# Turning and normalising the next block's rows later in a fused attention and mixture-of-experts kernel

## The reference

```python
scores = jnp.einsum('ti,ei->te', xt, gate_w)
probs = jax.nn.softmax(scores, axis=-1)
expert_weights, expert_indices = jax.lax.top_k(probs, NUM_ACT)
expert_weights = expert_weights / expert_weights.sum(axis=-1, keepdims=True)
x1 = jax.nn.silu(jnp.einsum('ti,eoi->teo', xt, w1))
x3 = jnp.einsum('ti,eoi->teo', xt, w3)
expert_outs_all = jnp.einsum('teo,eio->tei', x1 * x3, w2)
```

## Time and profile before

| | |
|---|---|
| median of 3 runs | 804.17 us (804.14 to 805.19) |
| profiled execution, its own time | 806.62 us |
| its span, first to last instruction | 804.9 us |
| mean granted TensorE clock | 0.945 of full speed |
| TensorE products busy | 729.1 us, 91% |
| VectorE busy | 412.8 us, 51% |
| ScalarE busy | 305.1 us, 38% |
| GpSimd busy | 172.6 us, 21% |

### The profile page before, as it was taken

How to read it: one execution, slowest core, us unless ns; L and a number is a source line. 1 busy time by engine, 2 the same in 40 slices (tenths; PEclk the granted TensorE clock), 3 DMA queues, 4 the chain that set the end, 5 groups by cost and what they waited for, 6 DMA issues and landing times.

```text
span 804.9 us, 10568 instructions
## 1 busy us (share of the span) xinstructions
PE 729.1 (91%) x3364; PEld 574.8 (71%) x3365; DVE 412.8 (51%) x1011; ACT 305.1 (38%) x497; POOL 172.6 (21%) x224
## 2 busy tenths in 40 slices
PE   7393089889999999999999999999999999999995
PEld 3193054566787888788887888888888888888884
DVE  3988977885382226522282256322832563274222
ACT  4754636711362126311272255211722452172121
POOL 2353001992111111111111111111121111111211
PEclk9755579999999999999999999999999999999998
DMA  8962043664174113711174228111652182111121
GB/s 290 389 245 104 0 181 136 223 224 136 33 252 129 27 26 105 260 26 26 26 230 151 37 39 323 30 26 26 192 186 39 27 324 41 26 26 26 33 39 34
DMA packets 23103, 94.52 MB, mean 117 GB/s; under 512 B 4336, under 2 KB 4592, under 8 KB 19248
## 3 DMA queue, kind: packets, MB, share of 16 engines
q1 hardware_dynamic: 14496, 70.54, 23.7%
q0 software_dynamic: 8448, 23.81, 14.5%
q10 hardware_dynamic: 144, 0.00, 0.0%
HBM read 74.02 MB, written 20.33 MB: 117 GB/s over the span
## 4 chain that ended last, share of the span: by engine, by line
issue 68%; DVE 14%; POOL 7%; PE 5%; POOLq 3%; DVEq 2%; DMA 1%; ACT 0%; SPq 0%
POOL out L482 5%; DVE front L1002 2%; POOL xtile L443 2%; PE bank L566 1%; POOLq L479 1%; POOLq L289 1%; DVE top L1104 1%; PE bank L575 1%; PE bank L526 1%; DVE ln_stats L960 1%; DVE front L1101 1%; DVE scratch L977 1%; PE bank L564 1%; DVE xb L1155 1%; DMA front<-ctxT 1%
## 5 line engine op out<-in xcount | busy, mean ns | idle before, releaser
L621 PE MATMUL bank<-w_hi,xT_hi 128*128 128x512 f32 x560 | 225.0, 402 | 0.6 <-DVE xT_lo L1344 0.6
L623 PE MATMUL bank<-w_lo,xT_hi 128*128 128x512 f32 x560 | 221.4, 395 | 0.0
L622 PE MATMUL bank<-w_hi,xT_lo 128*128 128x512 f32 x560 | 221.3, 395 | 0.0
L898 ACT ACTIVATE act_g<-bank 128x512 f32<-128x512 f32 x70 | 41.6, 594 | 279.1 <-PE bank L623 279.1
L623 PEld LDWEIGHTS bank<-w_lo,xT_hi 128*128 128x128 f32 x560 | 105.4, 188 | 25.4
L621 PEld LDWEIGHTS bank<-w_hi,xT_hi 128*128 128x128 f32 x560 | 105.5, 188 | 24.9 <-issue 0.8
L622 PEld LDWEIGHTS bank<-w_hi,xT_lo 128*128 128x128 f32 x560 | 105.6, 189 | 23.2
L621 PE MATMUL bank<-w_hi,hT_hi 128*128 128x512 f32 x280 | 115.8, 414 | 4.8 <-DVE hT_lo L1360 4.6
L1360 DVE TENSOR_TENSOR hT_lo<-bank,hT_hi 128x512 fp32r<-128x512 f32 x70 | 48.3, 690 | 125.6 <-ACT hT_hi L902 123.2
L1164 DVE TENSOR_TENSOR w_lo<-raw,w_hi 128x1024 fp32r<-128x1024 f32 x88 | 103.9, 1221 | 14.4 <-ACT w_hi L810 13.4
L623 PE MATMUL bank<-w_lo,hT_hi 128*128 128x512 f32 x280 | 109.7, 392 | 0.0
(11 more groups left out here) (227 smaller groups left out, 714.9 us busy)
## 6 DMA issues: line engine op xcount, KB each, us to landing
raw<-weights SPq DMA_DIRECT2D x24, 2048.0 KB, 7.6
xb<-x SPq DMA_DIRECT2D x4, 1024.0 KB, 13.1
raw<-xT SPq DMA_DIRECT2D x4, 1024.0 KB, 9.8
w_hi<-weights POOLq DMA_DIRECT2D x2, 2048.0 KB, 13.9
found<-xb SPq DMA_DIRECT2D x4, 1024.0 KB, 4.7
out<-xb SPq DMA_DIRECT2D x4, 1024.0 KB, 7.6
found<-scratch SPq DMA_DIRECT2D x1, 2092.0 KB, 30.1
front<-ctxT SPq DMA_DIRECT2D x4, 256.0 KB, 5.2
```

What stands on the lines that cost most here:

```text
L621: nc.tensor.matmul(out_ap, hi, hi_w, start=start, stop=False)
L622: nc.tensor.matmul(out_ap, lo, hi_w, start=False, stop=False)
L623: return nc.tensor.matmul(out_ap, hi, lo_w, start=False, stop=stop)
L898: nc.scalar.activation(act_g[:, s, :], bank[GATE[s]][:, :], ACT.Silu).then_inc(silu_set[s], 1)
```

## The change

On all three engines the loops' order is changed, and nothing is added or taken away. TensorE turns the next block's rows four chunks before the block's end (ahead of chunk 4, before its wait for `hT_set[1]`) instead of before chunk 0. ScalarE normalises them behind `h_high(0)` in a plain block (behind `h_high(1)` in a block of a change) instead of behind `silu(0)`, and makes x's high part behind `h_high(1)`. VectorE makes x's low part behind `h_low(1)`. In a block of a change some of the weights' splits change places with these.

```diff
                     for c in range(2, DC):
                         first_layer(1, 1, c).then_inc(piece_done[1], 1)
-                    transpose_x(nth + 1)
                     pe.wait_ge(hT_set[0], nth)
...
                     second_layer([2, 3]).then_inc(piece_done[2], 1)
+                    transpose_x(nth + 1)
                     pe.wait_ge(hT_set[1], nth)
...
                         silu(0, nth)
-                        normal_x(nth + 1)
                         fresh_high(0, 3, done)
...
                         h_high(0, nth)
                         fresh_high(1, 2, done)
+                        fresh_high(1, 3, done)
+                        h_high(1, nth)
+                        normal_x(nth + 1)
+                        act.wait_ge(raw_in[2], arrived)
+                        fresh_high(2, 0, done)
                         x_high(nth + 1)
-                        h_high(1, nth)
-                        fresh_high(1, 3, done)
-                        act.wait_ge(raw_in[2], arrived)
-                        for j in range(OPS):
+                        for j in range(1, OPS):
                             fresh_high(2, j, done)
                     with act.Else():
                         silu(0, nth)
-                        normal_x(nth + 1)
                         silu(1, nth)
                         h_high(0, nth)
+                        normal_x(nth + 1)
+                        h_high(1, nth)
                         x_high(nth + 1)
-                        h_high(1, nth)
...
                         product(1, nth, ups)
+                        split_low(1, e, [2])
+                        h_low(1, nth)
+                        split_low(1, e, [3])
                         x_low(nth + 1)
-                        h_low(1, nth)
-                        split_low(1, e, range(2, OPS))
-                        split_low(2, after, range(2))
+                        split_low(2, after, [0])
                         scale_y(e, g, ups)
                         take_meta()
-                        split_low(2, after, range(2, OPS))
+                        split_low(2, after, range(1, OPS))
                     with dve.Else():
                         product(0, nth, ups)
                         h_low(0, nth)
                         product(1, nth, ups)
+                        h_low(1, nth)
                         x_low(nth + 1)
-                        h_low(1, nth)
                         scale_y(e, g, ups)
```

## The result

The changed kernel is **slower**: 816.37 us (815.81 to 816.82, 4 runs) against 804.68 us for the kernel before (4 runs, 804.14 to 806.14: the three from before the prediction and one more). The ratio is 1.0142, with a 95% interval of 1.0124 to 1.0160, so 10 to 13 us. (In brackets behind a median stand the lowest and the highest time.) The forecast was 811.6, with a range up to 816.3; the median lies 0.07 us above that end, inside the 1 us by which the changed kernel's runs scatter.

What follows compares the result with a forecast made beforehand. TensorE, busy in 91% of the span, was taken as the bound. 33 blocks x 0.37 = 12.2 us, less 4.69 gained, is +7.5; against the timed median 804.17 that gave 811.6 us, range 808.7 to 816.3.

Steps and rivals of the forecast that it cites:

- Step 1: Ahead of the second layer: without the turns of x, TensorE newly waits 0.23 us for h_low(0), gaining only 0.13 a block.
- Step 2: Behind that new wait: slower steps up to the turning of h cost 0.04 us; h's second half waits for nothing.
- Step 3: At the turns' new place, four chunks from the block's end: interrupting the dense stream costs 0.46 us a block.
- The bound of 0.41: High end of the cost per block, in us, if steps behind the interruption are also 0.04 slower; 0.37 was taken.
- Step 4: At the next block's start: the later work on x still ends in time, slack 0.82 us, hence no stall.
- The gain: Blocks behind a change of expert: with normal_x behind h_high(0), late gathers delay nothing, so all 4.69 us go.
- Steps 5 and 6: Blocks of a change, and POOL and SP: reordered splits, scale_y up to 0.8 us and loads up to 1.2 earlier; no term.
- A: Faster: h_low(0) is in time and the turns cost no more at the new place; 799.5 us, chance 0.07.
- B: Smaller: turns disturb the dense stream less, 0.23 or 0.32 us a block; 804.1 or 807.1 us, chance 0.06.
- C: Slower still: x's low part misses the next block's start, stalling each block 0.36 us; 823.5 us, chance 0.04.
- D: Turns of x wait for normal_x behind very late gathers, losing part of 4.69 us; 816.3 at most; 0.83 including the forecast.

Runs made afterwards that it cites:

- idle turns: Kernel before with four unused, unwaited turns of h's first half added four chunks from the block's end: 819.75 us; with eight, one run: 832.81 us.
- the cure alone: Kernel before with only one VectorE edit: one split of group 2 instead of two ahead of scale_y in a block of a change; 801.57 us, ratio 0.9972.
- the two large sets later: The unchanged kernel before, timed again beside the follow-up runs: 804.28 us (17 runs) and 803.36 us (23 runs).
- the run with the late load: Changed kernel with group 1's last split behind x_low, so group 1's load starts later; normal_x stays behind h_high(0): 815.60 us.

## What held of the prediction, and where its sum was short

The direction was right, and so was the mechanism of the cost; the time came out 0.07 us above the upper end of the range. What removed the late gathers was not the move that the text named. Step by step:

- **Step 1** (without the turns, TensorE waits 0.23 us and chunk 0 starts 0.13 us sooner). Right: 11.96 to 11.83.
- **Step 2** (0.04 us slower steps behind the wait, and the turning of h "waits for nothing"). The first part was right, 0.80 us from 375.90 to 376.70. The second failed by a little: the turning starts on time and takes 0.40 us (376.70 to 377.10), where it took 0.35 before. h is ready at 376.63, only 0.07 us ahead of it, which is the likely reason. More important is what the step did not see, that h's second half bounds the place anyway. Had the wait for hT_lo not been there, the block would have lasted as long, as the run with h turned earlier showed.
- **Step 3** (the interruption costs 0.46 us). This is the mis-sized term of the sum. It measured 0.52 by idle turns in the kernel before, and in the changed kernel 3.21 - 2.72 = 0.49 behind the turns' start. I read the two steps beside the turns and left out that some nine behind them are slower by 0.005 each. The bound of 0.41 that I gave for a block was below the 0.45 that came.
- **Step 4** (no stall at the next block's start). Right, with 1.00 us of slack for 0.82.
- **The gain** (4.69 us go). Against the profiled execution it was right in size: all its 4.69 us of long blocks are gone. In timed runs it is smaller on the average, as the text allowed. The kernel with the cure alone takes 801.57 us, 3.1 us less than the 804.68 beside which the change was timed, and 1.8 to 2.7 less than the two large sets later. Its plain blocks are 0.03 us longer, 1.0 us in all, so without late gathers the kernel before would take some 800.6, near its fastest run, 800.82. That makes the gain 2.8 to 4.1 us by set, an estimate. The 2.45 us between the profiled execution and the timed median, which the text named, was a sign of this.
- **What the gain was credited to.** normal_x behind h_high(0) would have shielded TensorE, as the run with the late load shows. It was not needed: VectorE's reordered splits alone keep every gather in time.
- **The sum.** In the profiled executions it closes: 33 x 0.45 - 4.69 = 10.2 us, and 815.1 - 804.9 = 10.2. The forecast by the profiled execution was 814.1 and 816.79 came, of which the block is 33 x 0.08 = 2.6. For the medians, 14.8 - 4.1 = 10.7 of the measured 11.7. The rest, 1.0 us, is within what four runs of the kernel before leave open. That the median came so near the end of the range is in part chance: that end was made by giving up the whole gain, and the block term, which did grow, had been given 0.41 at most.
- **Steps 5 and 6** ("No term"). They noted that the next gather comes up to 0.8 us earlier and the loads of groups 0 and 1 up to 1.2, and took nothing for it. That alone was enough for the whole gain: the earlier load of group 1 in the changed kernel, the sooner scale_y in the kernel before.

Of the rivals, A fell on the turning of h and on step 3. B fell by the idle turns: 0.52 us and not 0.23 or 0.32. The Trainium skill (TensorE: Matmul & The Clock Gate, Back-to-back issue gap) has 81 ns or 56 ns for a product of 128 columns. That does not agree with this case, where four more turns take 0.44 us, 0.11 each, at a granted clock of 1.00; the measurement decides. C did not occur: xT_lo was ready 1.00 us ahead of the next block. Nor did D: TensorE has no wait for xtile in the loop.

## What to carry to other kernels

Work that stands where its engine would wait anyway costs less than it takes, and whoever moves it pays its full price at the new place. Before moving it, ask what the next two waits behind it are, not only the first: here the second bounded the saving at 0.10 us, against some 0.5 paid. When a cost shows only in some executions (a kernel that scatters by 5 us), look first at what else is being transferred around the late transfer, before it and behind it: one split moved behind scale_y gave 0.28%, while rebuilding the order of three engines around the lateness lost 1.4%.

## What was not expected of the hardware

- **A break in a dense stream of products is felt behind it.** Four turns take 0.44 us and cost 0.52. The eleven steps from 0.67 us behind the first turn on were spaced by 0.230 us and not 0.227. Behind eight turns they were spaced by 0.227. Why the slower steps are missing there stays open.
- **A wait that ends 0.07 us ahead of a product still costs 0.1 us.** h_low(1) ended at 268.54 and the product started on time at 268.61, but the step behind it came 0.33 us later. The load of the operand had waited until 268.60. The same operand ready 0.56 us ahead (h_low(1) ends at 266.74, the product starts at 267.30) gave 0.23.
- **Some tenths of a us decide whether a gather is late.** Issued 4.1 to 4.2 us behind the start of the load of group 1, with that of group 2 started 0.35 us behind the end of its own issue, the gather's rows came 6.6 to 11.3 us into a block, differently from block to block (the kernel before, and with four or eight idle turns). Issued 3.3 us behind the one, with its issue ended 1.5 us ahead of the other, they came at 7.5 to 7.7 (the cure). With 0.35 us again, but 5.7 us behind the start of the load of group 1, they came at 7.0 to 7.2. How the transfers share the queues to that effect stays open.
